# Feed forward of a transformer block: a normalization applied by GpSimd, copies by ScalarE, a loop written out, and the weighing matmuls in alternating order

## The chip, the cores and the metric

The kernel runs on one core of a Trainium2 chip. The metric is the device time in microseconds (us) of that core, the median of several executions. The profile was taken in one execution of its own; all single times below are from it.

## The reference, cut to what matters

```
x = x + layernorm(attn(layernorm(x)))          # attn: 16 heads of 64, over 2 x 2048 tokens of 256
x = x + layernorm(ffn(layernorm(x)))           # output: this is the last line

attn(x): q, k, v = x@Wq+bq, x@Wk+bk, x@Wv+bv
         ctx = softmax(q k^T / 8) v
         y = x + ctx@Wo + bo
         return (y-mean)*rsqrt(var+1e-3)*gamma + beta
ffn(x):  h = silu(x@wg^T) * (x@wu^T)           # 768 hidden
         return h@wd^T
layernorm(x) = (x - mean) / sqrt(var + 1e-5)
```

All tensors are float32. The kernel keeps float32 accuracy by splitting operands in a high and a low part and multiplying three of the four pairs.

## The kernel before

**Attention** comes first. For each of 2 batches and 16 heads it runs 64 steps (4 blocks of 512 queries, 16 tiles of 128 keys). A step has on TensorE one matmul for a coming block's maxima (line 754), two for the scores (766, 767), and the weighing of the values with the probabilities, `weigh`: for each quarter `q` of 128 queries three matmuls of 64 or 65 columns, high probabilities `p_h` by the values with a column of ones (line 787), `p_h` by the low part of the values (789), low probabilities `p_l` by the values (791). ScalarE makes the probabilities (lines 541, 542), GpSimd and VectorE their low parts (476, 606), VectorE the maxima (589). `weigh` is called for two steps at a time.

**Feed forward** comes second and works on 8 groups of 512 tokens. Each group passes through a *turn*; turns 0 to 7 follow each other and each overlaps three groups. Turn g does the following.
- Six hidden tiles f = 0 to 5: TensorE makes gate and up products (`ps_g`, `ps_u`), ScalarE the silu, VectorE their product `hf` (line 1248, called hf(0) to hf(5) below), ScalarE its high part `hTh` (1086), GpSimd its low part `hTl` (1134, hTl(0) to hTl(5)). Between them the attention output of group g+2 is turned (`cTh` by ScalarE, `cTl` by VectorE, line 1156), up to turn 5.
- Behind hf(0) and hf(1), VectorE normalizes the *output* of group g-1, which lies in `o_tok` (named `late` in the profile): moments, then twelve Newton steps on four numbers per partition (lines 89 to 96) and the application (x-mean)*root on 4 times 256 columns (`apply_root`, line 117). GpSimd then adds the residual (`residual`, line 1128) behind hTl(1), and SyncE stores the result.
- Behind hf(2) to hf(4), VectorE does the first normalization of group g+1: moments, Newton steps, gamma and beta. Behind hf(5) come its second and third normalization; TensorE multiplies by Wo and by wd meanwhile.
- At the end the turned normalized input is split (`nTh`, `nTl`, line 1237), the output is turned back into `ps_t`, and VectorE copies it to `o_tok` (line 1271).

Behind turn 7, `end` normalizes and stores the last group. Turns 1 to 4 are a hardware loop of two passes with two turns each; turns 0, 5, 6 and 7 are straight code. In the loop, waits depend on the group number, which each engine computes in registers. Every engine has its own queue and works it in the written order; semaphores tie them together. Turns 6 and 7 have no group to turn in.

`end_step` counts the steps of the output's normalization: 2 for the moments, 12 for Newton, 1 for the application, 15 (`NORM`) in all. `t_free` counts readings of the two banks of `ps_t`.

## Time and profile before

| | us |
|---|---|
| median of 3 runs | 3069.83 |
| lowest and highest run | 3065.18, 5660.74 |
| the profiled execution, its own time | 3067.56 |
| its span, first to last instruction | 3065.8 |
| mean granted TensorE clock | 0.977 of full speed |

Attention fills the span up to about 2627 us; the turns start at 2688.5 us, and turn 1 at 2735.48 us, taken at the first `nTl` of the turn before. The share of an engine's busy time is an average over both parts, and the matmuls' ends are modelled, so what an engine's time is worth has to be read in the stretch itself.

### The profile page before, as it was taken

To read this page: it belongs to the slowest core of one execution; us is meant where nothing else is said; L and a number is where in the kernel's file an instruction comes from. 1 tells how busy PE (TensorE), PEld (TensorE's weight loads), DVE (VectorE), ACT (ScalarE), POOL (GpSimd) and SP (SyncE) were. 2 spreads that over 40 slices of the span, in tenths; PEclk is the share of its full clock that TensorE was granted. 3 is DMA by queue.
4 is the path that set the end of the run, shared out by engine and by line. 5 is a ranking of instruction groups with operands and counts; after the bars stand their busy time and mean duration, and the time that the engine had idled before them with its cause. 6 is when DMAs were issued, how large, how long until landed. Compare 5 with 4: busy or idle time off the path is not lost. (4 is left out here: it accounts for less than half of the span.)

```text
span 3065.8 us, 83116 instructions
## 1 busy us (share of the span) xinstructions
PE 2901.0 (95%) x33632; PEld 2129.8 (69%) x33632; DVE 2590.7 (85%) x4729; ACT 2397.0 (78%) x4587; POOL 2308.8 (75%) x1810
## 2 busy tenths in 40 slices
PE   5799999999999999969999999999999999788996
PEld 4577777777777777656777777777777777577775
DVE  5688888888888888967888888888888888578886
ACT  3599999999999998947999999999998999432322
POOL 3588888888888888837888888888888888222222
PEclk8999999999999999989999999999999999799998
DMA  2623333333333333025333333333333331312110
GB/s 92 162 58 71 67 65 66 65 66 69 67 71 70 69 69 93 9 73 158 65 65 66 65 65 69 66 72 70 69 69 66 65 64 52 111 45 76 49 41 21
DMA packets 211660, 214.04 MB, mean 70 GB/s; under 512 B 158672, under 2 KB 181328, under 8 KB 198992
## 3 DMA queue, kind: packets, MB, share of 16 engines
q1 hardware_dynamic: 211280, 208.79, 28.9%
q8 instruction: 261, 4.28, 0.6%
q14 instruction: 119, 0.97, 0.1%
HBM read 53.16 MB, written 37.88 MB: 30 GB/s over the span
## 5 line engine op out<-in xcount | busy, mean ns | idle before, releaser
L476 POOL TENSOR_TENSOR p_l<-p_f,p_h 128x512 f16<-128x512 f32 x1536 | 1939.6, 1290 | 172.0 <-ACT p_h L542 164.4
L589 DVE TENSOR_REDUCE mx<-ps_aux 128x1 f32<-128x512 f32 x2048 | 1349.3, 681 | 246.2 <-PE ps_aux L754 242.3
L541 ACT ACTIVATE p_f<-ps_score 128x512 f32<-128x512 f32 x2048 | 1246.0, 609 | 88.6 <-PE ps_score L767 17.8
L542 ACT ACTIVATE p_h<-ps_score 128x512 f16<-128x512 f32 x2048 | 1254.4, 613 | 0.0
L766 PE MATMUL ps_score<-q_hilo,k_hihi 128*128 128x512 f32 x2048 | 1193.4, 583 | 1.4 <-ACT p_h L542 1.4
L787 PEld LDWEIGHTS ps_ctx<-v_hi_one_lo,p_h 128*128 128x128 f16 x8192 | 746.5, 96 | 286.6 <-issue 217.7
L787 PE MATMUL ps_ctx<-v_hi_one_lo,p_h 128*128 128x65 f16 x8192 | 873.6, 194 | 0.8 <-POOL p_l L476 0.8
L789 PE MATMUL ps_ctx<-v_hi_one_lo,p_h 128*128 128x64 f16 x8192 | 863.7, 195 | 0.0
L791 PE MATMUL ps_ctx<-v_hi_one_lo,p_l 128*128 128x65 f16 x8192 | 858.1, 192 | 0.0
L754 PE MATMUL ps_aux<-k_half,q_half 65*128 65x512 f16 x2048 | 809.3, 396 | 17.4 <-DVE mx L589 15.5
L767 PE MATMUL ps_score<-q_hi_max,k_lo_one 65*128 65x512 f32 x2048 | 815.1, 398 | 0.0
L789 PEld LDWEIGHTS ps_ctx<-v_hi_one_lo,p_h 128*128 128x128 f16 x8192 | 763.0, 97 | 0.0
L791 PEld LDWEIGHTS ps_ctx<-v_hi_one_lo,p_l 128*128 128x128 f16 x8192 | 762.6, 99 | 0.0
L606 DVE TENSOR_TENSOR p_l<-p_f,p_h 128x512 f16<-128x512 f32 x512 | 618.0, 1207 | 19.3 <-ACT p_h L542 19.3
L754 PEld LDWEIGHTS ps_aux<-k_half,q_half 65*128 65x128 f16 x2048 | 230.9, 113 | 310.8 <-issue 242.6
L767 PEld LDWEIGHTS ps_score<-q_hi_max,k_lo_one 65*128 65x128 f32 x2048 | 394.0, 192 | 52.9
L766 PEld LDWEIGHTS ps_score<-q_hilo,k_hihi 128*128 128x128 f32 x2048 | 422.8, 206 | 9.9 <-ACT p_h L542 8.7
L457 POOL TENSOR_TENSOR lo_st<-qk_new,hi_st 128x512 fp32r<-128x512 f32 x128 | 178.5, 1394 | 166.3 <-DVE hi_st L580 166.3
L1134 POOL TENSOR_TENSOR hTl<-late,hTh 128x512 fp32r<-128x512 f32 x48 | 63.2, 1317 | 276.2 <-ACT hTh L1086 276.1
L494 ACT ACTIVATE qk_new<-ps_aux,b_cur 128x512 f32<-128x512 f32 x128 | 87.9, 687 | 157.8 <-PE ps_aux L741 135.7
L465 POOL TENSOR_TENSOR p_f<-p_f,v_new 128x512 f32<-128x512 f32 x64 | 71.9, 1132 | 87.7 <-ACT v_new L525 87.4
L741 PE MATMUL ps_aux<-xTh,w_h 128*128 128x512 f32 x256 | 104.0, 406 | 7.2 <-ACT qk_new L494 4.2
(126 smaller groups left out, 2600.4 us busy)
## 6 DMA issues: line engine op xcount, KB each, us to landing
k_hihi<-hi_st SPq DMA_DIRECT2D x64, 512.0 KB, 8.7
v_heads<-v_new SPq DMA_DIRECT2D x64, 258.0 KB, 2.0
v_hi_one_lo<-v_heads SPq DMA_DIRECT2D x32, 516.0 KB, 9.0
q_hilo<-hi_st SPq DMA_DIRECT2D x32, 512.0 KB, 4.4
q_hilo<-lo_st SPq DMA_DIRECT2D x32, 512.0 KB, 6.6
q_hi_max<-hi_st SPq DMA_DIRECT2D x32, 512.0 KB, 4.7
k_lo_one<-lo_st SPq DMA_DIRECT2D x32, 512.0 KB, 6.8
heads<-ctx_n SPq DMA_DIRECT2D x128, 128.0 KB, 2.0
```

Of the source, the lines that this page charges most:

```text
L457: nc.gpsimd.tensor_tensor(lo_w[:, cols], qk_new[:, :], hi_st[:, cols], ALU.subtract)\
L476: nc.gpsimd.tensor_tensor(p_l[:, r], p_f[:, r], p_h[:, r], ALU.subtract).then_inc(lo_pool, 1)
L541: nc.scalar.activation(p_f[:, r], ps_score[:, bank], ACT.Exp, scale=K ** -0.5)
L542: nc.scalar.activation(p_h[:, r], ps_score[:, bank], ACT.Exp, scale=K ** -0.5).then_inc(exp_done, 1)
L589: nc.vector.reduce_max(mx[:, blk % 2, tt, ch:ch + 1], ps_aux[:, bank], AX_X).then_inc(max_read, 1)
L606: nc.vector.tensor_tensor(p_l[:, r], p_f[:, r], p_h[:, r], ALU.subtract).then_inc(lo_dve, 1)
L754: nc.tensor.matmul(ps_aux[:, bank], q, kM[u][:, ch * BLK:(ch + 1) * BLK], start=True, stop=True).then_inc(aux_full, 1)
L766: nc.tensor.matmul(ps_score[:, (g * STEPS + t) % RING], kA[u][:, keys], qA[u][:, cols], start=True, stop=False)
L767: nc.tensor.matmul(ps_score[:, (g * STEPS + t) % RING], kB[u][:, keys], qB[u][:, cols], start=False, stop=True).then_inc(s_full, 1)
L787: nc.tensor.matmul(acc, p_h[:, r, toks], v_one, start=(kt == 0 and q == 0), stop=False, skip_group_check=True)
L789: nc.tensor.matmul(acc[:, 0:K], p_h[:, r, toks], v_lo, start=False, stop=False, skip_group_check=True)
L791: mm = nc.tensor.matmul(acc, p_l[:, r, toks], v_one, start=False, stop=(kt == KT - 1 and q == TB - 1), skip_group_check=True)
```

## The change

Four edits:
- `apply_root` on the output leaves VectorE. GpSimd does it inside `residual`, with four `tensor_scalar` of 256 columns, as soon as the Newton steps are done (`end_step` at `ROOT`), then counts `end_step` up itself and adds the residual as before. The output's normalization has its own small tiles (`small_o`).
- The two copies from `ps_t` to `o_tok` at the end of each turn leave VectorE for ScalarE, with the waits they need; VectorE waits for them before the moments.
- Turns 1 to 4 are written out instead of looped.
- In `weigh`, the three matmuls of odd quarters come in reverse order.

```diff
--- before.py
+++ after.py
@@ -784,12 +784,12 @@
                     acc = ps_ctx[:, j % 2, q * (K + 1):(q + 1) * (K + 1)]
                     toks = slice(q * P, (q + 1) * P)
                     v_one, v_lo = V[u][:, kt, 0:K + 1], V[u][:, kt, K + 1:VW]
-                    nc.tensor.matmul(acc, p_h[:, r, toks], v_one, start=(kt == 0 and q == 0), stop=False,
-                                     skip_group_check=True)
-                    nc.tensor.matmul(acc[:, 0:K], p_h[:, r, toks], v_lo, start=False, stop=False,
-                                     skip_group_check=True)
-                    mm = nc.tensor.matmul(acc, p_l[:, r, toks], v_one, start=False,
-                                          stop=(kt == KT - 1 and q == TB - 1), skip_group_check=True)
+                    parts = [(acc, p_h, v_one), (acc[:, 0:K], p_h, v_lo), (acc, p_l, v_one)]
+                    if q % 2:
+                        parts.reverse()
+                    for n, (to, p, v) in enumerate(parts):
+                        mm = nc.tensor.matmul(to, p[:, r, toks], v, start=(kt == 0 and q == 0 and n == 0),
+                                              stop=(kt == KT - 1 and q == TB - 1 and n == 2), skip_group_check=True)
                 mm.then_inc(pv_done, 1)
 
 
@@ -892,6 +892,10 @@
             return 2 * FEED + DT + (G - 2) * TURN + 2 * DT
         return g * TURN + 2 * FEED + DT
 
+    def turn_items(g):
+
+        return (FEED if g < G - 2 else 0) + (DT if g < G - 1 else 0) + DT
+
     def feed_at(f):
 
         return range(f * CT // FT, (f + 1) * CT // FT)
@@ -930,6 +934,9 @@
         st2 = sb("st2", [P, TB, 6], F32)
         mv2 = sb("mv2", [P, TB, 2], F32)
         small = (st2, mv2, *(sb(f"norm2_{k}", [P, TB], F32) for k in range(3)))
+        st3 = sb("st3", [P, TB, 6], F32)
+        mv3 = sb("mv3", [P, TB, 2], F32)
+        small_o = (st3, mv3, *(sb(f"norm3_{k}", [P, TB], F32) for k in range(3)))
 
         const_loaded = sem("const_loaded")
         w_loaded = [wo_loaded] + [sem(f"w_loaded{k}") for k in range(1, 4)]
@@ -979,11 +986,8 @@
             feed(1, 1)
             chain(0, 0)
             turn(0, 0, True, True, True)
-            with eng.Fori(0, (G - 4) // 2) as i:
-                g = eng.snap(i * 2 + 1)
-                turn(g, 1, False, True, True)
-                turn(g + 1, 0, False, True, True)
-            turn(G - 3, 1, False, True, True)
+            for g in range(1, G - 2):
+                turn(g, g % 2, False, True, True)
             turn(G - 2, 0, False, False, True)
             turn(G - 1, 1, False, False, False)
             end(G - 1, 1)
@@ -1103,6 +1107,13 @@
                     nc.scalar.activation(oT[:, c], ps_y[:, c], ACT.Copy).then_inc(o_read, 1)
                 if chains:
                     high_normed(g + 1, base + (FEED if feeds else 0))
+                item = base + turn_items(g) - DT
+                act.wait_ge(res_ready, g + 1)
+                act.wait_ge(t_free, item + 2)
+                for c in range(2):
+                    act.wait_ge(t_full, item + c + 1)
+                    nc.scalar.activation(o_tok[:, 2 * c:2 * c + 2], ps_t[:, c].rearrange("p (t d) -> p t d", d=D),
+                                         ACT.Copy).then_inc(t_free, 1)
 
             walk(act, feed, nothing, turn, nothing)
 
@@ -1124,6 +1135,12 @@
                 nc.gpsimd.tensor_tensor(xn[:, :, :], xn[:, :, :], stat(x_root), ALU.mult).then_inc(xn_ready, 1)
 
             def residual(g, u):
+                _, mv, _, y, _ = small_o
+                pool.wait_ge(end_step, g * NORM + ROOT)
+                for t in range(TB):
+                    ins = nc.gpsimd.tensor_scalar(o_tok[:, t], o_tok[:, t], mv[:, t, 0:1], y[:, t:t + 1],
+                                                  ALU.subtract, ALU.mult)
+                ins.then_inc(end_step, 1)
                 pool.wait_ge(end_step, (g + 1) * NORM)
                 nc.gpsimd.tensor_tensor(x1[u][:, :, :], x1[u][:, :, :], o_tok[:, :, :], ALU.add)\
                     .then_inc(res_ready, 1)
@@ -1204,14 +1221,16 @@
             def norm_x1(g, u):
                 norm(nc, dve, xn2, x1[u], EPS_LN, small, chain_step, g * CHAIN + 2 * ROOT + 3)
 
-            def last_norm(g, u):
-                norm(nc, dve, o_tok, o_tok, EPS_LN, small, end_step, g * NORM)
-
             def last_moments(g, u):
-                moments(nc, dve, o_tok, small, end_step, g * NORM)
-
-            def last_scale(g, u):
-                scale(nc, dve, o_tok, o_tok, EPS_LN, small, end_step, g * NORM)
+                dve.wait_ge(t_free, turn_base(g) + turn_items(g) + 2)
+                moments(nc, dve, o_tok, small_o, end_step, g * NORM)
+
+            def last_newton(g, u):
+                newton(nc, dve, EPS_LN, small_o, end_step, g * NORM + MOMENTS)
+
+            def last_root(g, u):
+                last_moments(g, u)
+                last_newton(g, u)
 
             def feed(g, u):
                 if g == 0:
@@ -1251,28 +1270,19 @@
                         for k in feed_at(f):
                             lo_c(g + 2, k)
                     if f < 2 and not first:
-                        (last_moments, last_scale)[f](g - 1, 1 - u)
+                        (last_moments, last_newton)[f](g - 1, 1 - u)
                     if 2 <= f < 5 and chains:
                         (moments_z, newton_z, gamma_beta)[f - 2](g + 1, 1 - u)
                 if chains:
                     root_again(g + 1, 1 - u)
                     first_residual(g + 1, 1 - u)
                     norm_x1(g + 1, 1 - u)
-                item = base
                 if feeds:
                     add_x(g + 2, base + CT)
-                    item = base + FEED
                 if chains:
                     low_normed(g + 1)
-                    item = item + DT
-                dve.wait_ge(res_ready, g + 1)
-                for c in range(2):
-                    dve.wait_ge(t_full, item + c + 1)
-                    nc.vector.tensor_copy(o_tok[:, 2 * c:2 * c + 2],
-                                          ps_t[:, c].rearrange("p (t d) -> p t d", d=D)).then_inc(t_free, 1)
-                dve.wait_ge(t_free, item + DT + 2)
-
-            walk(dve, feed, chain, turn, last_norm)
+
+            walk(dve, feed, chain, turn, last_root)
 
         @block.tensor
         def _(pe):
```

GpSimd in turn 5, before (`late<-late` of 128x1024 and `x_0<-x_0,late` are the residual's addition) and of the change:

```order
L1134 TENSOR_TENSOR hTl<-late,hTh 128x512 x2
L1128 TENSOR_TENSOR x_0<-x_0,late 128x1024
L1134 TENSOR_TENSOR hTl<-late,hTh 128x512 x4
L1121 TENSOR_TENSOR xn<-x_t,x_mean 128x1024
L1124 TENSOR_TENSOR xn<-xn,x_root 128x1024
```

```order
L1151 TENSOR_TENSOR hTl<-late,hTh 128x512 x2
L1141 TENSOR_SCALAR late<-late,mv,norm_1 128x256 x4
L1145 TENSOR_TENSOR x_0<-x_0,late 128x1024
L1151 TENSOR_TENSOR hTl<-late,hTh 128x512 x4
L1132 TENSOR_TENSOR xn<-x_t,x_mean 128x1024
L1135 TENSOR_TENSOR xn<-xn,x_root 128x1024
```

Four scalings have come in front of the addition, between hTl(1) and hTl(2); the rest of the order stands.

ScalarE from the end of turn 5 into turn 6, before and of the change (`late<-ps_g` is the silu, `late<-ps_y` the output product):

```order
L1050 ACTIVATE yT<-ps_y,bo_c 128x512 x2
L1103 ACTIVATE late<-ps_y 128x512 x2
L1077 ACTIVATE nTh<-ps_t 128x512 x2
L1092 ACTIVATE late<-ps_g 128x512 x2
L1086 ACTIVATE hTh<-late 128x512
```

```order
L1054 ACTIVATE yT<-ps_y,bo_c 128x512 x2
L1107 ACTIVATE late<-ps_y 128x512 x2
L1081 ACTIVATE nTh<-ps_t 128x512 x2
L1115 ACTIVATE late<-ps_t 128x512 x2
L1096 ACTIVATE late<-ps_g 128x512 x2
L1090 ACTIVATE hTh<-late 128x512
```

The two copies stand between the last `nTh` and the first silu of the next turn.

TensorE in attention, the first `weigh` of a pair, before and of the change:

```order
L787 MATMUL ps_ctx<-v_hi_one_lo,p_h 128x65
L789 MATMUL ps_ctx<-v_hi_one_lo,p_h 128x64
L791 MATMUL ps_ctx<-v_hi_one_lo,p_l 128x65
L787 MATMUL ps_ctx<-v_hi_one_lo,p_h 128x65
L789 MATMUL ps_ctx<-v_hi_one_lo,p_h 128x64
```

```order
L791 MATMUL ps_ctx<-v_hi_one_lo,p_h 128x65
L791 MATMUL ps_ctx<-v_hi_one_lo,p_h 128x64
L791 MATMUL ps_ctx<-v_hi_one_lo,p_l 128x65 x2
L791 MATMUL ps_ctx<-v_hi_one_lo,p_h 128x64
L791 MATMUL ps_ctx<-v_hi_one_lo,p_h 128x65 x2
```

The low probabilities of two neighbouring quarters now stand side by side, and so do the high ones by the values with ones; the number of matmuls is the same.

## Rows read from the trace of the kernel before

**Rows 1.** The page, part 1: busy time, share, instructions.

```profile
PE 2901.0 (95%) x33632; PEld 2129.8 (69%) x33632; DVE 2590.7 (85%) x4729; ACT 2397.0 (78%) x4587; POOL 2308.8 (75%) x1810
```

**Rows 2.** Windows, attention: stretch, its us, busy us of PE, PEld, DVE, ACT, POOL, clock.

```profile
1240.00:1260.00 20.00, 20.00 (x274) 14.24 (x273) 19.22 (x29) 19.00 (x38) 17.62 (x14) 1.00 0.04 9
```

**Rows 3.** Timeline of attention: start, duration, engine, line.

```profile
1501.58 0.21 PE L787 MATMUL ps_ctx<-v_hi_one_lo,p_h 128*128 128x65 f16 x1
...
1502.33 0.38 PE L754 MATMUL ps_aux<-k_half,q_half 65*128 65x512 f16 x1
...
1503.75 0.21 PE L787 MATMUL ps_ctx<-v_hi_one_lo,p_h 128*128 128x65 f16 x1
```

**Rows 4.** The page, part 5: the three weighing matmuls of each quarter.

```profile
L787 PE MATMUL ps_ctx<-v_hi_one_lo,p_h 128*128 128x65 f16 x8192 | 873.6, 194 | 0.8 <-POOL p_l L476 0.8
...
L789 PE MATMUL ps_ctx<-v_hi_one_lo,p_h 128*128 128x64 f16 x8192 | 863.7, 195 | 0.0
...
L791 PE MATMUL ps_ctx<-v_hi_one_lo,p_l 128*128 128x65 f16 x8192 | 858.1, 192 | 0.0
```

**Rows 5.** Windows: turns 1 to 4 together, then turn 5.

```profile
2735.48:2933.87 198.39, 178.28 (x848) 143.63 (x848) 165.68 (x500) 60.56 (x105) 56.20 (x36) 0.97 0.18 64
2933.87:2982.36 48.49, 43.14 (x212) 34.73 (x212) 42.76 (x125) 15.33 (x27) 14.04 (x9) 1.00 0.04 11
```

**Rows 6.** Timeline of VectorE in turn 5; in brackets idle time before.

```profile
2938.67 0.69 DVE L1248 TENSOR_TENSOR late<-ps_u,late 128x512 f32<-128x512 f32 x1 [2.07 <-PE ps_u L1289]
...
2943.53 1.28 DVE L89 TENSOR_SCALAR norm<-mv 128x4 f32<-128x4 f32 x1
...
2947.02 2.36 DVE L117 TENSOR_SCALAR late<-late,mv,norm 128x256 f32<-128x256 f32 x4
...
2949.41 0.69 DVE L1248 TENSOR_TENSOR late<-ps_u,late 128x512 f32<-128x512 f32 x1
...
2955.87 1.28 DVE L96 SCALAR_TENSOR_TENSOR norm<-norm,norm 128x4 f32<-128x4 f32 x1
...
2957.78 0.69 DVE L1248 TENSOR_TENSOR late<-ps_u,late 128x512 f32<-128x512 f32 x1
...
2967.07 0.95 DVE L89 TENSOR_SCALAR norm<-mv 128x4 f32<-128x4 f32 x1
...
2968.26 1.74 DVE L91 TENSOR_SCALAR norm<-norm 128x4 int32<-128x4 int32 x1
```

**Rows 7.** Timeline of GpSimd in turn 5.

```profile
2947.16 1.42 POOL L1134 TENSOR_TENSOR hTl<-late,hTh 128x512 fp32r<-128x512 f32 x1 [2.38 <-ACT hTh L1086]
...
2949.46 2.38 POOL L1128 TENSOR_TENSOR x<-x,late 128x1024 f32<-128x1024 f32 x1 [0.88 <-DVE late L117]
...
2952.65 1.29 POOL L1134 TENSOR_TENSOR hTl<-late,hTh 128x512 fp32r<-128x512 f32 x1 [0.81 <-ACT hTh L1086]
...
2955.83 1.29 POOL L1134 TENSOR_TENSOR hTl<-late,hTh 128x512 fp32r<-128x512 f32 x1 [1.89 <-ACT hTh L1086]
...
2966.10 1.89 POOL L1121 TENSOR_TENSOR xn<-x_t,x_mean 128x1024 f32<-128x1024 f32 x1
...
2968.08 1.90 POOL L1124 TENSOR_TENSOR xn<-xn,x_root 128x1024 f32<-128x1024 f32 x1
```

**Rows 8.** Timeline of VectorE in turn 2, inside the loop.

```profile
2794.72 0.69 DVE L1248 TENSOR_TENSOR late<-ps_u,late 128x512 f32<-128x512 f32 x1 [0.39 <-DVE mv L74]
```

**Rows 9.** Timeline of ScalarE at the start of turn 5.

```profile
2937.36 0.60 ACT L1092 ACTIVATE late<-ps_g 128x512 f32<-128x512 f32 x1 [2.92 <-PE ps_g L1289]
```

**Rows 10.** Timeline of VectorE in turn 6.

```profile
2994.37 1.38 DVE L117 TENSOR_SCALAR late<-late,mv,norm 128x256 f32<-128x256 f32 x4
...
3002.81 0.69 DVE L1248 TENSOR_TENSOR late<-ps_u,late 128x512 f32<-128x512 f32 x1
```

**Rows 11.** Timeline of VectorE in turn 7 and behind it.

```profile
3042.10 0.69 DVE L1248 TENSOR_TENSOR late<-ps_u,late 128x512 f32<-128x512 f32 x1 [2.54 <-POOL hTl L1134]
...
3058.58 1.38 DVE L117 TENSOR_SCALAR late<-late,mv,norm 128x256 f32<-128x256 f32 x4
```

## The prediction

> **What bounds the kernel now.** I read the page first, then windows by stage, then timelines of single turns. TensorE is busy 95% of the span, VectorE 85%, ScalarE 78% and GpSimd 75% [rows 1], but that is an average over two parts with different limits.
>
> In attention TensorE never stops: 20.00 us of 20, with VectorE at 19.22 and ScalarE at 19.00 close behind [rows 2]. A pair of steps takes 2.17 us (1501.58 to 1503.75), of which the 24 weighing matmuls take 0.75 us (1501.58 to 1502.33), about 31 ns each [rows 3]. So anything that the new order does to a weighing matmul counts in full: 3 times 8192 of them [rows 4] make 24,576, and one nanosecond on each is 25 us.
>
> In the feed forward the bound is VectorE's chain. In turn 5 it waits 2.07 us for the first product of TensorE [rows 6] and then works almost without a gap: 42.76 of 48.49 us are busy [rows 5], and what looks busy is partly stalled. The Newton steps work on four columns; one lasts about 0.2 us (three steps between 2957.15 and 2957.78), yet the one at 2955.87 lasts 1.28 us [rows 6]. It ends at 2957.15, just after GpSimd's hTl(3) (2955.83 + 1.29 = 2957.12) [rows 7]. The same at 2967.07 and 2968.26 (0.95 and 1.74 us), which end with GpSimd's two operations at 2966.10 and 2968.08; between those two, two small VectorE steps got through [rows 6, 7]. The 2.36 us of the application at 2947.02 have hTl(1) of 2947.16 inside them; without a neighbour four such operations take 1.38 us [rows 6, 7, 10]. So small VectorE steps and GpSimd exclude each other, and more work on GpSimd is not free even when GpSimd has time. The products `hf` and `cTl`, which read PSUM, and the moments run beside it unhindered.
>
> On the rule behind this: the Trainium skill, "SBUF — State Buffer", section "Who interferes with whom", says that a VectorE instruction with two SBUF inputs or in a two-port mode and a GpSimd instruction that reads SBUF exclude each other for the whole instruction. By that rule the four new scalings, which the trace doesn't show, would block as the subtractions do; here they fall beside `hf`, `cTl` and moments, and the sum is the same with or without it.
>
> **The application moves to GpSimd, turns 1 to 5.** I play turn 5 again. Newton for the output ends at 2947.02, so hf(2) starts there and not at 2949.41 [rows 6]: 2.37 us gained. GpSimd: hTl(1) starts at 2947.16, undisturbed 1.29 us, ends 2948.45; four scalings of a us each, end 2948.45 + 4a; addition 2.38; hTl(2) 1.29; hTl(3) 1.29 (its input, 2955.83 before, comes 2.37 earlier, at 2953.46, in time). GpSimd is thus busy without a gap until 2953.41 + 4a [rows 7]. VectorE's next Newton chain, which now would start 2.37 us earlier, at about 2951.9, runs into this: its first steps slip in one or two at a time between GpSimd's operations, as above, and some nine of twelve are left when hTl(3) ends. They take 1.8 us, so hf(4) starts at 2955.2 + 4a, against 2957.78. The turn changes by 4a - 2.57. What follows hf(4) keeps its distances on all engines; the tail of the turn is shared by VectorE's chain and TensorE's products, and both hang on the last `cTl`, so the shift reaches the next turn whole.
>
> The price a has no row. Near ones: a subtraction with a repeated operand takes 1.89 us for 1024 columns, a quarter of it is 0.47; an addition takes 2.38 for 1024 and hTl 1.29 for 512, which carried on to 256 columns gives 1.29 - 0.545 = 0.75 [rows 7]. One tensor is read instead of two, which speaks for the lower end, and an instruction has a fixed part that is paid four times, which speaks for the upper. I take the middle, 0.6. Five turns then give 5 x (2.4 - 2.57) = -0.85 us; the bounds give -3.45 and +2.15.
>
> The Trainium skill, "GPSIMD Engine Reference", section "3.1 Elementwise — side-by-side cycle accounting", states some 1.8 cycles of 1.2 GHz per element for a tight one-input loop; my estimate from that page is 0.38 us for 256 columns, and the sum below would be -9.6 us. No run here shows this operation yet.
>
> **Turn 6, turn 7 and the end.** In turn 6 hf(2) no longer waits for the application either (from 2994.37, 1.38 us), but GpSimd is then busy for 4a + 2.38 + 1.29 + 1.29 and nine Newton steps follow: 2994.37 + 4.96 + 1.8 + 4a = 3001.1 + 4a against 3002.81 [rows 10]: 4a - 1.7, so +0.7 (bounds +0.2 and +1.3). In turn 7 hf(4) waits 2.54 us for GpSimd [rows 11], and there the application lies on GpSimd's path: 4a against 1.4, +1.0 (+0.5, +1.6). Behind turn 7 nothing covers it: the application at 3058.58 took 1.38 us [rows 11], again +1.0 (+0.5, +1.6).
>
> **The copies move to ScalarE.** They leave VectorE where it then waits 2.07 us for TensorE [rows 6], so they cost it nothing now. ScalarE has 2.92 us idle before the first silu [rows 9], and two operations of 0.60 us fit in. Queued behind its new wait is that silu, which waits for TensorE anyway. If this cover were gone, 1.2 us a turn would show. At the end, where the copy is on the path, an operation of 0.60 replaces one of about 0.69 with a hand-over more. I count nothing.
>
> **The loop is written out.** Four looped turns take 198.39 us, a straight one 48.49 [rows 5]: 198.39 - 4 x 48.49 = 4.4 us. The kind of time that goes is seen at 2794.72, where hf(1) comes 0.39 us after its forerunner, with registers computed between [rows 8]; hf in turn 5 has no such gap [rows 6]. The bounds are nothing and 4.4: GpSimd's hits on Newton steps also differ between turns, and are not the loop's.
>
> **The weighing order.** Same matmuls, same weight loads, same waits ahead of them. By place in the triple they last 194, 195 and 192 ns [rows 4]. I take zero. Bounds: half of the triples are reversed, 12,288 matmuls; if each changed by the largest of these differences, 3 ns, it would be 37 us either way.
>
> **The sum.** -4.4 - 0.85 + 0.7 + 1.0 + 1.0 = -2.6 us (-6.7 with a = 0.47, +2.2 with a = 0.75). Against the profiled execution's own 3067.56 that is 3065.0; this execution lay 2.27 us under the median of the runs, 3069.83, so I forecast 3067 for a median. What a measurement of this kernel can tell from no change is 2%, 61 us; the forecast is far inside it.
>
> **Rivals.**
> - *The new order makes weighing faster*, up to 37 us: 3030 to 3055, say 3045. For it: TensorE is the bound, and ScalarE leaves 1 us in 20 of room [rows 2], 5%, so nothing caps so small a gain. Against it: no row shows a cost of one place. 10%.
> - *It makes weighing slower*, by the same mechanism and price, 3080 to 3104. 8%.
> - *GpSimd's scaling is dear*, the kernel slower than before. If its fixed part rules and 256 columns cost what hTl's 512 do, a = 1.29, then turns 1 to 5 give +2.6 each, turn 6 +3.5, turn 7 and the end +3.8 each: 13 + 3.5 + 7.6 - 4.4 = +19.7, or 3089. All terms together are 32a - 21.75, so the change loses from a = 0.68 on. For it: two operations and two pointers per instruction, of which no row is there. Against: none of GpSimd's rows has a fixed part near that size. 10%.
> - *The scaling is cheap*, a = 0.38. As a mechanism of this kernel: half the columns and half the tensors of hTl, 1.29 / 4 = 0.32 us, is the least that rows suggest, and between it and 0.47 lies 0.38; GpSimd's run then ends 0.9 us earlier in each turn than in my case, 32 x 0.38 - 21.75 = -9.6, or 3060. 15%, inside my case's range.
> - *Writing out brings nothing*, since what the loop's registers cost is taken again by GpSimd's hits: 3072. 5%.
>
> **Chances.** My case together with the last two, 3056 to 3074: 72%. Range 3046 to 3086: it takes in the nearer half of the faster and slower weighing and leaves the dear scaling's far end out. Faster by over 2% (under 3008): 2%. Slower by over 2% (over 3131): 2%. Within: 96%.
>
> **What would show it.** Right: GpSimd has 32 scalings of 0.5 to 0.75 us, VectorE 32 fewer at line 117; hf(2) comes some 2.4 us earlier after hf(0), but hf(4) at most 1 us earlier, with a Newton step of over 1 us before it under GpSimd's hTl(2) and hTl(3); turns 1 to 4 take 192 to 195 us; the pair of attention steps stays at 2.17 us. Wrong: if attention ends (the first `cTh`) more than 5 us from its place before, the order of weighing matters and my zero is the error; if hf(4) moves 2 us earlier, the exclusion costs less than I say; a turn above 49 us means a dear scaling.

## The result: slower by 0.4%, and the profile after

| | before | after |
|---|---|---|
| median, us | 3065.63 (7 runs from 3064.84) | 3078.39 (7 runs, 3077.04 to 3080.28) |
| ratio to before, 95% interval | | 1.004 [1.003, 1.005] |
| the profiled execution, its own time | 3067.56 | 3080.09 |
| its span | 3065.8 | 3078.3 |
| mean granted TensorE clock | 0.977 | 0.973 |

The three runs of the first table are among the seven before, the one of 5660.74 us too, and the ratio leaves that one out. The forecast, 3067, was 2.8 us below the median that it started from; the kernel is 12.8 us above the median measured beside it. The time lies inside the range, and the sign is wrong.

The page, part 1, of the kernel after; it answers to [rows 1]:

```profile
PE 2903.7 (94%) x33632; PEld 2132.7 (69%) x33632; DVE 2585.7 (84%) x4681; ACT 2406.7 (78%) x4603; POOL 2347.1 (76%) x1842
```

GpSimd has gained 32 operations and 38.3 us, VectorE has lost 48 operations and only 5.0 us. In the feed forward, from 2640 us on, it has lost nothing: 332.0 us busy before, 332.2 after. The 16.0 us of applications and 10.4 us of copies are gone there, but the Newton steps, whose stalls count as busy, take 118.3 us instead of 93.1. Where the span grew is seen in windows from one first `nTl` to the next: turns 1 to 5, turn 6, then turn 7 with the end. They answer to [rows 5].

```profile
2735.68:2785.37 49.69, 43.83 (x212) 35.99 (x212) 42.71 (x119) 16.24 (x29) 18.59 (x13) 0.97 0.18 64
2785.37:2835.63 50.26, 44.34 (x212) 36.60 (x212) 42.60 (x119) 16.18 (x29) 18.55 (x13) 0.93 0.19 63
2835.63:2886.32 50.69, 44.80 (x212) 36.92 (x212) 42.60 (x119) 16.14 (x29) 18.57 (x13) 0.93 0.18 63
2886.32:2937.29 50.97, 45.06 (x212) 37.08 (x212) 42.60 (x120) 16.15 (x29) 18.57 (x13) 0.93 0.18 63
2937.29:2986.87 49.58, 43.84 (x212) 35.94 (x212) 42.60 (x120) 16.23 (x29) 18.58 (x13) 0.97 0.03 11
2986.87:3028.50 41.63, 30.22 (x124) 23.19 (x124) 34.24 (x109) 10.46 (x18) 15.14 (x11) 0.91 0.04 13
3028.50:3078.30 49.80, 30.34 (x124) 23.59 (x124) 14.23 (x50) 11.11 (x19) 21.99 (x16) 0.81 0.06 21
```

Turn 1 starts 0.2 us later than before, so attention and turn 0 together have no part in it. Turns 1 to 4 take 201.6 us against 198.39, although the loop with its computed registers is gone; turn 5 takes 1.1 us more; and what lies behind turn 5 takes 91.4 us against 83.4 (3065.8 less 2982.36). Together +12.3 us.

The groups by line, GpSimd from 2640 us on, give the price that had no row:

```profile
L1141 POOL TENSOR_SCALAR late<-late,mv,norm 128x256 f32<-128x256 f32 x32 | 38.8, 1227 | 13.5 <-DVE norm L96 13.4
```

One scaling of 256 columns takes 1.227 us, nearly the 1.29 us of an `hTl` of 512 columns [rows 7]. In the timelines of turn 3, GpSimd first and VectorE second, line 1267 is `hf`, 1173 `cTl`, 1145 the addition and 1151 `hTl`:

```profile
2848.93 1.30 POOL L1151 TENSOR_TENSOR hTl<-late,hTh 128x512 fp32r<-128x512 f32 x1 [2.38 <-ACT hTh L1090]
2850.21 4.85 POOL L1141 TENSOR_SCALAR late<-late,mv,norm 128x256 f32<-128x256 f32 x4
2855.14 2.38 POOL L1145 TENSOR_TENSOR x<-x,late 128x1024 f32<-128x1024 f32 x1
2857.47 2.48 POOL L1151 TENSOR_TENSOR hTl<-late,hTh 128x512 fp32r<-128x512 f32 x2
```

```profile
2853.64 0.23 DVE L89 TENSOR_SCALAR norm<-mv 128x4 f32<-128x4 f32 x1
2853.91 0.50 DVE L90 TENSOR_SCALAR norm<-norm 128x4 int32<-128x4 int32 x1
2854.44 0.17 DVE L91 TENSOR_SCALAR norm<-norm 128x4 int32<-128x4 int32 x1
...
2855.23 2.30 DVE L93 TENSOR_TENSOR norm<-norm 128x4 f32<-128x4 f32 x1
2857.57 1.18 DVE L94 SCALAR_TENSOR_TENSOR norm<-norm,norm 128x4 f32<-128x4 f32 x1
2858.79 1.19 DVE L96 SCALAR_TENSOR_TENSOR norm<-norm,norm 128x4 f32<-128x4 f32 x1
...
2860.60 0.69 DVE L1267 TENSOR_TENSOR late<-ps_u,late 128x512 f32<-128x512 f32 x1
```

Read the second against the first. Three more steps stand where the first dots are: six Newton steps finish between 2853.64 and 2855.20, most of them while the scalings run (until 2855.06), at 0.16 to 0.50 us each. The next one starts just behind the addition's start and ends with it (2857.53), and the two behind it end with an `hTl` each. Then three steps are left, and `hf`(4) comes at 2860.60. So additions and `hTl` shut VectorE's small steps out, and scalings hardly do.

Windows of the kernel after around that `hf`(4), columns as above:

```profile
2850.00:2855.00 5.00, 5.00 (x27) 4.14 (x26) 4.78 (x18) 2.66 (x5) 5.00 (x5) 1.00 0.00 0
2855.00:2860.60 5.60, 2.24 (x12) 1.62 (x10) 5.32 (x9) 1.37 (x3) 4.87 (x4) 0.99 0.27 94
2860.60:2866.00 5.40, 4.06 (x12) 3.38 (x13) 5.37 (x10) 1.12 (x2) 1.27 (x1) 0.50 0.31 74
```

TensorE stands idle for 3.4 of the 5.6 us ahead of `hf`(4), and in the 5.4 us behind it is granted 0.50 of its clock, 1.2 instead of 2.4 GHz. `hf`(4) comes 1.1 to 2.2 us later in its turn than in the straight turns with the application on VectorE (25.0 against 22.8 to 23.9 us from the first `nTl`, e3 and e4 below), and the turn is some 2 us longer.

What the clock adds to that can be seen from turn to turn. In all five, `hf`(4) comes 24.9 to 25.1 us and `hf`(5) 30.6 to 30.7 us behind the first `nTl`. From `hf`(5) to the end of the turn it is 18.95 us in turns 1 and 5, as in every turn of e4 below (18.9), but 19.6, 20.0 and 20.3 us in turns 2, 3 and 4. The 10 us behind `hf`(4) in turn 1, in turn 3 and in turn 1 of e4 have the same VectorE time; the granted clock is 0.83, 0.66 and 1.00:

```profile
2760.73:2770.73 10.00, 8.65 (x34) 7.25 (x35) 9.85 (x23) 2.44 (x4) 4.16 (x3) 0.83 0.58 210
2860.60:2870.60 10.00, 8.66 (x29) 7.15 (x30) 9.85 (x23) 1.75 (x3) 4.16 (x3) 0.66 0.59 211
```

```profile
2757.61:2767.61 10.00, 7.80 (x36) 6.17 (x36) 9.85 (x23) 3.03 (x5) 4.23 (x3) 1.00 0.56 210
```

Turns 2 and 4 have 0.71 and 0.66 there, turn 5 has 0.83. So the wait is paid for once more in turns 2 to 4, with 0.7 to 1.4 us each, and not in turns 1 and 5.

Behind turn 5 nothing covers GpSimd. Its timeline in turn 7 and at the end:

```profile
3042.98 4.84 POOL L1141 TENSOR_SCALAR late<-late,mv,norm 128x256 f32<-128x256 f32 x4 [0.71 <-DVE norm L96]
3047.91 2.39 POOL L1145 TENSOR_TENSOR x<-x,late 128x1024 f32<-128x1024 f32 x1
...
3067.64 4.84 POOL L1141 TENSOR_SCALAR late<-late,mv,norm 128x256 f32<-128x256 f32 x4 [12.01 <-DVE norm L96]
3072.56 2.34 POOL L1145 TENSOR_TENSOR late<-late 128x1024 f32<-128x1024 f32 x1
```

And VectorE's `hf`(4) in turn 7, which waited 2.54 us for GpSimd before [rows 11]:

```profile
3051.66 0.69 DVE L1267 TENSOR_TENSOR late<-ps_u,late 128x512 f32<-128x512 f32 x1 [7.09 <-POOL hTl L1151]
```

4.84 us of scalings stand in both places where VectorE took 1.38 [rows 11].

### The profile page after: what moved, and what is told of

Its sections match the earlier page's. It is cut to its first block and busy times, and to the rows that moved or that the text cites. A ratio compares the mean times of both kernels' runs of the same rounds, so it can differ in the third digit from the quotient of the medians.

```text
span 3078.3 us, 82399 instructions
## 1 busy us (share of the span) xinstructions
PE 2903.7 (94%) x33632; PEld 2132.7 (69%) x33632; DVE 2585.7 (84%) x4681; ACT 2406.7 (78%) x4603; POOL 2347.1 (76%) x1842
## 5 line engine op out<-in xcount | busy, mean ns | idle before, releaser
L541 ACT ACTIVATE p_f<-ps_score 128x512 f32<-128x512 f32 x2048 | 1242.2, 607 | 89.3 <-PE ps_score L767 17.5
L791 PEld LDWEIGHTS ps_ctx<-v_hi_one_lo,p_h 128*128 128x128 f16 x16384 | 812.3, 98 | 287.6 <-issue 221.6
L791 PE MATMUL ps_ctx<-v_hi_one_lo,p_h 128*128 128x65 f16 (+1 forms) x16384 | 938.1, 195 | 0.8 <-POOL p_l L476 0.8
L791 PE MATMUL ps_ctx<-v_hi_one_lo,p_l 128*128 128x65 f16 x8192 | 793.9, 193 | 0.0
L606 DVE TENSOR_TENSOR p_l<-p_f,p_h 128x512 f16<-128x512 f32 x512 | 619.2, 1209 | 19.4 <-ACT p_h L542 19.3
L791 PEld LDWEIGHTS ps_ctx<-v_hi_one_lo,p_l 128*128 128x128 f16 x8192 | 531.6, 98 | 0.0
L1049 ACT ACTIVATE cTh<-ps_t 128x512 fp32r<-128x512 f32 x64 | 37.4, 597 | 83.7 <-PE ps_t L1316 83.7
L741 PE MATMUL ps_aux<-xTl,w_h 128*128 128x512 f32 x256 | 102.2, 399 | 0.0
```

The source lines that it names most:

```text
L541: nc.scalar.activation(p_f[:, r], ps_score[:, bank], ACT.Exp, scale=K ** -0.5)
L606: nc.vector.tensor_tensor(p_l[:, r], p_f[:, r], p_h[:, r], ALU.subtract).then_inc(lo_dve, 1)
L741: mm = nc.tensor.matmul(ps_aux[:, bank], w[:, c], t[:, c, cols], start=(m == 0), stop=(m == len(parts) - 1))
L791: mm = nc.tensor.matmul(to, p[:, r, toks], v, start=(kt == 0 and q == 0 and n == 0), stop=(kt == KT - 1 and q == TB - 1 and n == 2), skip_ ...
```

## The experiments

Two theories stood at the start. **Price**: all of the loss is the four scalings of a block, by their length, through the end of GpSimd's run and `hf`(4) in turns 1 to 5, and in full behind it. **Elsewhere**: a part of it comes from the copies on ScalarE or from the new order, and the written-out loop is worth less than thought. All kernels, with turns from first `nTl` to first `nTl` in the profiled execution (before: 246.9, 40.5, 42.9 us):

| kernel | median us (runs) | ratio to before, interval | turns 1-5 | turn 6 | turn 7, end |
|---|---|---|---|---|---|
| after | 3078.39 (7) | 1.004 [1.003, 1.005] | 251.2 | 41.6 | 49.8 |
| e1, order alone | 3065.07 (11) | 1.000 [0.9991, 1.0009] | 248.1 | 40.1 | 42.2 |
| e3, loop alone | 3056.98 (6) | 0.9972 [0.9960, 0.9984] | 240.6 | 40.1 | 42.4 |
| e4, after, VectorE applies | 3058.80 (7) | 0.9975 [0.9963, 0.9986] | 241.3 | 40.5 | 42.3 |
| e7, after, ScalarE applies | 3057.37 (7) | 0.9968 [0.9957, 0.9980] | 235.6 | 40.8 | 44.5 |
| e11, ScalarE, then VectorE | 3056.39 (5) | 0.9966 [0.9952, 0.9979] | 235.5 | 40.2 | 43.2 |
| e6, scalings twice | 3100.77 (4) | 1.0121 [1.0104, 1.0138] | 266.8 | 45.5 | 58.6 |
| e8, two wide operations | 3073.20 (10) | 1.003 [1.002, 1.004] | 250.6 | 42.0 | 48.1 |
| e9, scalings later | 3075.57 (6) | 1.0033 [1.0021, 1.0046] | 248.3 | 42.4 | 53.1 |
| e10, constants | 3068.89 (1) | | 249.9 | 41.5 | 47.5 |
| e12, one wide scaling | 3074.93 (1) | | 249.7 | 41.8 | 46.4 |
| e13, one operation | 3071.32 (1) | | 249.9 | 41.9 | 46.2 |

Turn 0 takes 45.1 to 47.0 us from one kernel to the next, and the first `nTl` of turn 0 stands between 2681.9 (e6) and 2691.4 us (e1, e3), so single times are worth less than the turns. The turns scatter too: e1 has the same feed forward as the kernel before, and its turns 1 to 5 take 1.3 us more, its turns 6 and 7 with the end 1.1 us less. Of all turns together (330.5 against 330.3 us) little is left of that.

**e1, the order alone.** The kernel before with this edit:

```diff
-                    nc.tensor.matmul(acc, p_h[:, r, toks], v_one, ...)
-                    nc.tensor.matmul(acc[:, 0:K], p_h[:, r, toks], v_lo, ...)
-                    mm = nc.tensor.matmul(acc, p_l[:, r, toks], v_one, ...)
+                    parts = [(acc, p_h, v_one), (acc[:, 0:K], p_h, v_lo), (acc, p_l, v_one)]
+                    if q % 2:
+                        parts.reverse()
```

> The kernel before, with only the order of the three weighing matmuls of odd quarters reversed. Theory A (the dear scaling on GpSimd makes the loss, 1.23 us for 256 columns in the trace of the change, and the order costs nothing): 3065.6 us as before, within 1.5 us. Theory B (the order costs something in attention, where the change's trace stands 1.9 us later at the first cTh): 3067.5 us if all of these 1.9 us are its, and 3070 or more if it also carries a part of the rest.

Measured: 1.000 with 0.0009 to either side, some 3 us. The order is worth nothing that this measurement can tell, and the 37 us that the rivals gave it are excluded.

**e3, the loop alone.** The kernel before with this edit:

```diff
-            with eng.Fori(0, (G - 4) // 2) as i:
-                g = eng.snap(i * 2 + 1)
-                turn(g, 1, False, True, True)
-                turn(g + 1, 0, False, True, True)
-            turn(G - 3, 1, False, True, True)
+            for g in range(1, G - 2):
+                turn(g, g % 2, False, True, True)
```

> The kernel before, with only turns 1 to 4 written out. Theory A: what the straight turn 5 saves against the looped ones, 4.4 us, so 3061.2 us; turns 1 to 4 together 194 us in place of 198.4. Theory C (writing out brings nothing, because the stalls of VectorE behind GpSimd fill the room): 3064 to 3067 us, turns 1 to 4 at 197 us or more.

Measured: 0.9972. Turns 1 to 4 take 192.6 us against 198.39, so 5.8 us in the turns, or 7.6 against the looped turns of e1 (200.2); by the ratio it is 8.6 us (4.9 to 12).

**e4, the application back on VectorE**, the rest as after:

```diff
-                pool.wait_ge(end_step, g * NORM + ROOT)
-                for t in range(TB):
-                    ins = nc.gpsimd.tensor_scalar(o_tok[:, t], ...)
-                ins.then_inc(end_step, 1)
...
                 newton(nc, dve, EPS_LN, small_o, end_step, g * NORM + MOMENTS)
+                apply_root(nc, dve, o_tok, o_tok, small_o, end_step, g * NORM)
```

> The change with the application of the output's normalization back on VectorE; the copies stay on ScalarE, the loop stays written out, the order stays alternating. Theory A (only the scaling on GpSimd costs): the sum of a neutral copy, a neutral order and the straight loop, 3061 us, and turn 7 with what follows it back from 49.8 to 43 us. Theory D (the copies on ScalarE cost too, through the first silu of the next turn or a hand-over at the end): 3064 us or more with nTl to hf(0) longer than in the straight turn before, 4.8 us.

Measured: 0.9975, and turn for turn within 0.5 us of e3. Since e4 differs from e3 in the copies and the order, both together cost nothing that shows: 0.9 us by the windows from turn 1 on (324.0 against 323.1), less than the turns scatter. Since after differs from e4 in the application alone, the application costs 1.004 - 0.9975 = 0.0065, 20 us, and by the two intervals 5 us more or less; the turns say 9.9 + 1.2 + 7.5 = 18.6. "Elsewhere" is out.

**e6, each scaling twice**, the first time into a tile that nobody reads:

```diff
+                for t in range(TB):
+                    nc.gpsimd.tensor_scalar(extra[:, t], o_tok[:, t], mv[:, t, 0:1], y[:, t:t + 1],
+                                            ALU.subtract, ALU.mult)
                 for t in range(TB):
                     ins = nc.gpsimd.tensor_scalar(o_tok[:, t], ...)
```

> The change with every scaling on GpSimd issued twice (the first time into a spare tile), 4.9 us more work on GpSimd per group. If the length of GpSimd's run before hTl(2) and hTl(3) sets hf(4): the Newton steps are all done by then and hf(4) waits for hTl(2) alone, so a turn grows by 4.9 - 1.8 = 3.1 us in turns 1 to 6 and by 4.9 in turn 7 and at the end: 3078.4 + 28 = 3106 us. If scalings also hold VectorE's Newton steps for their whole length, 4.9 us in each of the eight places: 3117 us.

Measured: +22.4 us over after. By the windows from turn 1 on it is +28.3 us (15.6 in turns 1 to 5, 3.9 and 8.8 behind them), just the 28 of the first theory; in the profiled execution of e6 turn 0 began 8.7 us earlier than in that of after. The groups of GpSimd, and VectorE's timeline in turn 3:

```profile
L1142 POOL TENSOR_SCALAR extra<-late,mv,norm 128x256 f32<-128x256 f32 x32 | 38.7, 1225 | 13.7 <-DVE norm L96 13.7
L1145 POOL TENSOR_SCALAR late<-late,mv,norm 128x256 f32<-128x256 f32 x32 | 38.6, 1223 | 0.0
```

```profile
2852.95 0.16 DVE L94 SCALAR_TENSOR_TENSOR norm<-norm,norm 128x4 f32<-128x4 f32 x1
...
2853.36 0.34 DVE L93 TENSOR_TENSOR norm<-norm 128x4 f32<-128x4 f32 x1
...
2854.57 0.34 DVE L96 SCALAR_TENSOR_TENSOR norm<-norm,norm 128x4 f32<-128x4 f32 x1
2861.74 0.69 DVE L1271 TENSOR_TENSOR late<-ps_u,late 128x512 f32<-128x512 f32 x1 [6.83 <-POOL hTl L1155]
```

The whole chain of twelve passes beside the scalings at 0.16 to 0.49 us a step, and VectorE then waits 6.83 us for GpSimd. So what decides here is when GpSimd's run ends, not that scalings stop VectorE.

**e7, ScalarE applies**, as root x value + bias. VectorE makes the bias in one more small step, ScalarE takes the four operations behind `hTh`(1), or behind the last step at the end:

```diff
+                nc.vector.scalar_tensor_tensor(out=w[:, :], in0=mv[:, :, 0], scalar=-1.0, in1=y[:, :],
+                                               op0=ALU.mult, op1=ALU.mult).then_inc(end_step, 1)
...
+                    ins = nc.scalar.activation(o_tok[:, t], o_tok[:, t], ACT.Identity, bias=w[:, t:t + 1],
+                                               scale=y[:, t:t + 1])
```

> The change with the application on ScalarE: (x-mean)*root is made as root*x + (-mean*root), one more small VectorE step, four activations of 256 columns behind hTh(1). Theory A (GpSimd's 4.9 us per group are the cost, VectorE's 2.4 us the possible gain, and ScalarE shares no port with either): hf(4) about 1.7 us earlier than in the straight turn before in turns 1 to 5, turn 6 about 1 us shorter, turn 7 and the end even, written-out loop 4.4: 3065.6 - 4.4 - 9.5 = about 3052 us. Theory E (TensorE's work behind hf(5) or its clock sets the turn, not VectorE's chain): turns stay at 48.5 us and the time near 3061.

Measured: 0.9968. An operation takes 0.592 us, `hf`(4) comes 22.4 us after the first `nTl` instead of 25.0, and turns 1 to 5 take 15.6 us less than after and 5.7 less than e4. Turn 6, turn 7 and the end give 2.6 us of it back to e4. The expectation was 5 us too low.

**e8, two operations of 1024 columns** with a repeated operand in place of the four scalings; the second waits for the first by a semaphore:

```diff
-                for t in range(TB):
-                    ins = nc.gpsimd.tensor_scalar(...)
+                nc.gpsimd.tensor_tensor(o_tok[:, :, :], o_tok[:, :, :], wide(mv[:, :, 0:1]), ALU.subtract)...
+                nc.gpsimd.tensor_tensor(o_tok[:, :, :], o_tok[:, :, :], wide(y[:, :].unsqueeze(2)), ALU.mult)...
```

> The change with GpSimd's application as two operations of 1024 columns with repeated operands (subtract, multiply; 1.9 us each by the rows of its neighbours), 3.9 us in place of 4.9. If the Newton steps pass during the scalings but not during such operations, some nine steps are left behind hTl(3), turns 1 to 5 stay even, and only turn 7 and the end gain 0.95 us each: 3076.5 us. If GpSimd's run length alone decides, 8 x 0.95 us are gained: 3070.8 us.

Measured: 1.003, 3073.2 us, between the two numbers. GpSimd's groups:

```profile
L1142 POOL TENSOR_TENSOR late<-late,mv 128x1024 f32<-128x1024 f32 x8 | 15.2, 1898 | 13.4 <-DVE norm L96 13.4
L1144 POOL TENSOR_TENSOR late<-late,norm 128x1024 f32<-128x1024 f32 x8 | 15.2, 1894 | 0.6
```

A block takes 3.8 us instead of 4.9, yet turns 1 to 5 gain 0.6 us in all, less than they scatter; turn 7 and the end gain 1.7. VectorE's timeline in turn 3 shows why:

```profile
2850.61 0.17 DVE L90 TENSOR_SCALAR norm<-norm 128x4 int32<-128x4 int32 x1
2850.81 2.25 DVE L91 TENSOR_SCALAR norm<-norm 128x4 int32<-128x4 int32 x1
2853.10 1.19 DVE L93 TENSOR_TENSOR norm<-norm 128x4 f32<-128x4 f32 x1
2854.32 1.18 DVE L94 SCALAR_TENSOR_TENSOR norm<-norm,norm 128x4 f32<-128x4 f32 x1
```

GpSimd is done earlier, but fewer steps got through ahead of the addition. Seven are left behind `hTl`(3) instead of three, and `hf`(4) comes only 0.2 us earlier.

**e9, the scalings and the addition later**, behind `hTl`(3):

```diff
-                    if f == 1 and not first:
+                    if f == 3 and not first:
                         residual(g - 1, 1 - u)
```

> The change with scalings and addition moved behind hTl(3), from behind hTl(1). If the loss in turns 1 to 5 is hf(4) waiting behind GpSimd's run (4.7 us of TensorE idle in turn 3), turns fall to about 47 us and the time to about 3062 us, with turn 7 and the end unchanged. If it is the exclusion between the two engines wherever the scalings stand, gamma and beta are stalled instead, turns stay at 49 us or more and the time at 3074 or more.

Measured: 1.0033. `hf`(4) did come 0.8 to 3.4 us earlier, but turns 2 to 5 are no shorter than 49.5 us, with `hf`(0) 1.4 to 2.6 us later in them, and turn 7 with the end takes 3.3 us more than after. The theory that only the wait for `hf`(4) counts fell here. GpSimd and VectorE in turn 4 of e9:

```profile
2903.68 6.20 POOL L1141 TENSOR_SCALAR late<-late,mv,norm 128x256 f32<-128x256 f32 x4
2909.97 2.40 POOL L1145 TENSOR_TENSOR late<-late 128x1024 f32<-128x1024 f32 x1
2912.32 2.54 POOL L1151 TENSOR_TENSOR hTl<-late,hTh 128x512 fp32r<-128x512 f32 x2
2914.82 1.90 POOL L1132 TENSOR_TENSOR xn<-x_t,x_mean 128x1024 f32<-128x1024 f32 x1
```

```profile
2905.48 1.67 DVE L1198 SCALAR_TENSOR_TENSOR z<-z,mv,gam 128x256 f32<-128x256 f32 x4
2907.18 1.69 DVE L1203 SCALAR_TENSOR_TENSOR z<-z,norm,bet 128x256 f32<-128x256 f32 x4
...
2912.56 1.08 DVE L89 TENSOR_SCALAR norm<-mv 128x4 f32<-128x4 f32 x1
2913.67 1.22 DVE L90 TENSOR_SCALAR norm<-norm 128x4 int32<-128x4 int32 x1
2914.93 1.82 DVE L91 TENSOR_SCALAR norm<-norm 128x4 int32<-128x4 int32 x1
```

Now the scalings are stretched themselves, 6.20 us instead of 4.85, under VectorE's wide operations, and GpSimd's run stands on the chain's second Newton, whose steps take 1.08 to 1.82 us. The same collision has moved to another chain.

**e10, e12 and e13, what makes the price.** Each leaves a part of the output's normalization out: e10 subtracts 0 and multiplies by 1, e12 does the same in one instruction of 1024 columns, e13 multiplies only (by 1 or, in every other instruction, by the root).

```diff
-                    ins = nc.gpsimd.tensor_scalar(o_tok[:, t], o_tok[:, t], mv[:, t, 0:1], y[:, t:t + 1],
+e10                 ins = nc.gpsimd.tensor_scalar(o_tok[:, t], o_tok[:, t], 0.0, 1.0,
                                                   ALU.subtract, ALU.mult)
+e12             nc.gpsimd.tensor_scalar(o_tok[:, :, :], o_tok[:, :, :], 0.0, 1.0, ALU.subtract, ALU.mult)
+e13                 ins = nc.gpsimd.tensor_scalar(o_tok[:, t], o_tok[:, t], y[:, t:t + 1] if t % 2 else 1.0, None, ALU.mult)
```

> The change with the constants 0 and 1 in place of the two pointers in GpSimd's scalings, so the output's last normalization is left unapplied. It prices the operation: if the pointers make it dear, 256 columns take 0.5 to 0.8 us in place of 1.23; if two operations per column or a fixed part do, they stay at 1.1 to 1.25 us.

> The changed kernel with the four scalings of a block as one GpSimd instruction of 128x1024 with constants 0 and 1 in place of mean and root, so the normalization is not applied. The kernel with constants and four instructions of 256 columns took 1.073 us each, 4.29 us a block. If this price goes by columns, the one instruction takes about 4.3 us. If most of it is fixed per instruction and its columns cost what those of GpSimd's two-tensor operations do (2.1 ns each, from 1.29 us at 512 and 2.38 us at 1024 columns), it takes 1.073 + 768 x 0.0021 = 2.7 us or less.

> The changed kernel with the subtraction left out of GpSimd's scalings: each of the four does one multiplication, two of them by the constant 1, two by the root through its pointer; the mean is not subtracted. With both operations one instruction of 256 columns took 1.07 us with constants and 1.23 us with pointers. If the price lies in the two operations, one operation takes 0.22 us fixed plus half of 0.85, 0.65 us, and 0.73 us with a pointer. If it lies in the form, whatever it computes, they take 1.07 and about 1.15 us.

The groups of GpSimd, one fence for each kernel in this order:

```profile
L1141 POOL TENSOR_SCALAR late<-late 128x256 f32<-128x256 f32 x32 | 33.4, 1073 | 13.4 <-DVE norm L96 13.4
```

```profile
L1140 POOL TENSOR_SCALAR late<-late 128x1024 f32<-128x1024 f32 x8 | 29.1, 3638 | 13.4 <-DVE norm L96 13.4
```

```profile
L1141 POOL TENSOR_SCALAR late<-late,norm 128x256 f32<-128x256 f32 x16 | 14.9, 929 | 0.0
L1141 POOL TENSOR_SCALAR late<-late 128x256 f32<-128x256 f32 x16 | 13.6, 853 | 13.4 <-DVE norm L96 13.4
```

From 256 to 1024 columns the price grows by 2.565 us: 3.34 ns a column and 0.22 us fixed. GpSimd's operation on two tensors costs 2.13 ns a column ((2.38 - 1.29) / 512) and 0.20 us fixed. Of the 1.227 us, then, if the fixed part is the same with one operation as with two, 0.22 are fixed, 0.15 are the two pointers (1.227 - 1.073; one pointer 0.929 - 0.853 = 0.08), 0.22 the second operation (1.073 - 0.853), and 0.63 are what one operation on 256 columns costs above the fixed part, 2.5 ns a column. Both expectations of e12 and of e13 missed, and the measured prices lie between the two: the price has no single cause, and most of it goes by columns.

What a shorter block did to the turns is seen across these kernels. A block is the four scalings or what stands for them, its time the sum of its instructions; steps are those of the Newton chain that were left in turn 3 when `hTl`(3) ended; `hf`(4) is counted from the first `nTl` of turn 3:

| kernel | block, us | steps left | `hf`(4) | turns 1-5 |
|---|---|---|---|---|
| e6 | 9.8 | 0 | 28.0 | 266.8 |
| after | 4.9 | 3 | 25.0 | 251.2 |
| e10 | 4.3 | 5 | 24.7 | 249.9 |
| e8 | 3.8 | 7 | 24.8 | 250.6 |
| e12 | 3.6 | 7 | 24.6 | 249.7 |
| e13 | 3.6 | 8 | 24.6 | 249.9 |

From 4.9 to 3.6 us a block, GpSimd's run ends 1.3 us earlier, but each step that no longer passes during it comes behind it, and `hf`(4) gains only 0.4 us. Turns 1 to 5 with the cheapest block still take 8.6 us more than e4. Turn 7 with the end, where nothing is left to pass, falls from 49.8 to 46.2 us.

**e11, ScalarE in turns 1 to 5, VectorE behind them.** As e7, but ScalarE's part is limited as shown, and VectorE takes the four operations of the other groups itself:

```diff
+    BY_ACT = G - 3
...
+                    if f == 2 and not first and g - 1 < BY_ACT:
+                        apply_o(g - 1, 1 - u)
```

> The changed kernel with the output's normalization applied by ScalarE in turns 1 to 5 and by VectorE in turns 6 and 7 and at the end. If the turns' gain and the end's loss of the kernel with ScalarE throughout are local to their turns, turns 1 to 5 stay at 47.0 to 47.3 us as there, and turn 6 with turn 7 and the end goes back from 85.3 to the 82.7 us of the kernel with VectorE throughout: 3053.4 us span, 2.6 us under the kernel with ScalarE throughout. Rival: what ScalarE gains in turns 1 to 5 comes back as a wait in turn 6, which then starts with VectorE behind: turn 6 with turn 7 and the end at 85 us, 3056 us.

The group by line, ScalarE from 2640 us on:

```profile
L1089 ACT ACTIVATE late<-late,norm,norm 128x256 f32<-128x256 f32 x20 | 10.4, 592 | 0.6
```

Turns 1 to 5 keep e7's 47.0 to 47.2 us each. Turn 6, turn 7 and the end take 83.4 us, between the 82.7 hoped for and e7's 85.3. 3056.39 us is the best median here and beats both kernels, 0.9966 of before, but the intervals of e3, e4, e7 and e11 overlap. By the windows e11 is 4.2 us ahead of e3 (318.9 against 323.1 us from turn 1 on); the medians can't tell that.

## Why the prediction was wrong

**The step that failed is the price a of a GpSimd scaling.** I took 0.6 us from bounds 0.47 to 0.75; it takes 1.227 us. My own sum, 32a - 21.75, gives +17.5 with it, where the profile shows +12.3; a second step, below, makes the difference. Both bounds were slopes of operations on two tensors, at most 2.13 ns a column, and "one tensor is read instead of two, which speaks for the lower end" was the error in them: even one operation on one tensor costs 2.5 ns a column, two cost 3.3, and the pointers add 0.15 us. I looked for dearness in a fixed part and found none; rightly, it is 0.22 us. The columns were dear. I had no row of this instruction on this engine, and gave bounds from other instructions as if they were bounds.

**The rival "dear scaling" was the case**, with a close to its 1.29 and 3089 us for it, which was 10.6 us too high. Its price rows were the wrong ones (a fixed part), and its sum, +19.7, is 7 us above the +12.3 of the profile, by the step below.

**The exclusion.** That additions and `hTl` shut out small VectorE steps held: 2.30, 1.18 and 1.19 us, each ending with one of them. That about nine steps would be left behind `hTl`(3) whatever the price did not: in turn 3 three are, because six went through ahead of the addition, most beside the scalings. `hf`(4) comes 1.1 us later than in turn 5 of the kernel before, where 4 x 1.227 - 2.57 makes 2.3. Nor does what follows `hf`(4) "keep its distances": in turns 2 to 4 the turn loses another 0.7 to 1.4 us behind `hf`(5), at the lower clock. The two errors nearly cancel: 11.7 us by the formula for turns 1 to 5, 9.9 measured against e4, of which 6.6 are `hf`(5) coming later and 3.2 lie behind it. That this sum comes out near is luck: for the block of 3.6 us of e13 the formula gives 5.0 against e4's 8.6.

The Trainium skill, "SBUF — State Buffer", section "Who interferes with whom", has a VectorE instruction with two SBUF inputs and a GpSimd instruction that reads SBUF exclude each other for the whole instruction. The trace agrees for the addition (a step of 2.30 us under one of 2.38) and disagrees for the scaling: e6 shows such steps at 0.16 to 0.34 us under scalings of 1.22. The Trainium skill, "GPSIMD Engine Reference", section "3.1 Elementwise — side-by-side cycle accounting", gave my estimate of 0.38 us for 256 columns; e13's simplest form measures 0.853, and the scaling 1.227.

**Turn 6, turn 7 and the end.** By the formula +3.2 and twice +3.5; measured against e4 +1.2 and +7.5. In turn 7 and at the end the mechanism was right and only a was off; e12 and e13 bear it out, with +4.2 and +3.9 against e4 where the formula gives 4.5 and 4.3. In turn 6 I overrated it, again by the steps that pass: there all twelve are done when `hTl`(3) ends, and `hf`(4) follows at once.

**The loop.** -4.4 was forecast; turns 1 to 4 show -5.8 (-7.6 against e1) and the medians -8.6 (-4.9 to -12). That writing out saves this much is shown; what in the loop costs it is not taken apart. In the looped turns of the kernel before `hf`(1) comes 8.7 to 9.5 us from the first `nTl` where e3 has 8.3, and from `hf`(5) to the end it is 19.3 us against 18.9. The term was a little small, since turn 5 of the kernel before, my measure of a straight turn, took 48.49 us where straight turns take 48.03 in four of e3's five. The traces show where that 0.46 us lies. In turn 5 before, `hTl`(3) ran into the Newton chain and held one step for 1.28 us [rows 6, 7]. In turn 3 of e3 it starts only at 2856.66, when the chain is done and `hf`(4) has started (2855.88), since TensorE and with it `hTh`(3) came later there:

```profile
2856.66 1.29 POOL L1131 TENSOR_TENSOR hTl<-late,hTh 128x512 fp32r<-128x512 f32 x1 [3.50 <-ACT hTh L1083]
```

`hf`(4) comes 1.1 us earlier, `hf`(5) 0.46 us, and from there to the end of the turn both take 18.94 us. Without this gain the change would have shown some 6 us more of loss.

**The copies and the order.** Both counted at nothing; e4 beside e3, and e1, show nothing.

**`hf`(2).** It came 2.4 us earlier (13.15 against 15.54 us from the first `nTl`), as forecast. It bought nothing, because `hf`(4) waits for GpSimd's run and came later all the same. In e7, where ScalarE does the scaling, the same gain at `hf`(2) shortens the turns.

**My own signs.** "A turn above 49 us means a dear scaling" is what turned up in all five turns, and turns 1 to 4 took 201.6 us in place of 192 to 195. The pair of attention steps stayed at 2.16 us (1501.58 to 1503.74), and Newton steps of over 1 us stand before `hf`(4), as forecast.

## What to carry to other kernels

When work moves to an engine that has no row of that instruction, the price is unknown, and the nearest rows don't bound it: an instruction with one tensor can cost more a column than one with two. Work out the break-even price (0.68 us by my sum) and ask how far the guess may be off before the sign turns: here 0.08 us, and it was off by 0.63. The break-even itself isn't shown: no run has a scaling under 0.85 us, and down to there turns 1 to 5 hardly got shorter. A run that another chain slips through in pieces has no fixed slope: what the run saves, the chain may still have to do behind it. An early finish on one chain is worth nothing if the run of the receiving engine ends the next one: count to the end of that run. And a wait on TensorE's inputs can cost more behind it in granted clock, here 0.7 to 1.4 us in three turns of five and nothing in the other two.

## What the runs showed of the hardware

- GpSimd on 256 columns of f32 from SBUF: 0.853 us for one operation with a constant, 0.929 with a pointer, 1.073 for two with constants, 1.227 with pointers; 3.638 us for 1024 columns and two constants. Two operations of 1024 columns with a repeated operand do the same in 3.8 us instead of 4.9. ScalarE does the four in 2.1 us (0.592 each, overlapping), VectorE in 1.38 when left alone.
- VectorE's four-column steps pass beside GpSimd's scalings (0.16 to 0.50 us), but not beside its additions and subtractions on whole tiles, whether the step reads one tensor (line 91, 2.25 us in e8) or two (line 93, 2.30 us). In the other direction four scalings took 6.20 us instead of 4.85 while VectorE's `gamma` and `beta` operations ran (e9). Why one form gives way and the other doesn't stays open.
- In turn 3, after 3.4 us without work in 5.6, TensorE was granted 0.50 of its clock for 5.4 us. In turn 1 the same wait was followed by 0.70 in 5.6 us (2760.70 to 2766.30). In e3, windows of turn 3 show 2.1 us idle in one window, with the clock at 0.91 there and at 0.75 in the next:

```profile
2847.00:2852.00 5.00, 2.87 (x13) 2.10 (x12) 4.92 (x13) 1.25 (x3) 3.30 (x3) 0.91 0.00 0
2852.00:2856.90 4.90, 4.90 (x20) 3.92 (x20) 4.45 (x20) 1.76 (x4) 1.40 (x2) 0.75 0.31 107
```

No run here holds the clock fixed. The comparison of turns with the same `hf`(4) and `hf`(5) and a different clock is the nearest to it: 0.83 and 0.66 to 0.71 in the 10 us behind `hf`(4), and 0.7 to 1.4 us between them. Why the same wait got a different clock stays open.
